# ScalarE begins the transfer of the negated maxima; a transpose, the second statistics and the variance, and one Rsqrt move forward; the maxima of two banks in one reduction

## The chip, the cores and the metric

The kernel runs on one core of a Trainium2 chip. The metric is the device time of one execution in microseconds (us). Five engines work side by side, each in the order of its own program, and wait for one another through semaphores: TensorE (PE in the rows; PEld is its weight load), VectorE (DVE), ScalarE (ACT), GpSimd (POOL) and SyncE (SP), which here does nothing but begin DMA transfers.

## What is computed

The input is `x` of 4 images x 96 channels x 128 x 128, float32. Two layers follow one another. The first is a window attention beside a depthwise convolution:

```python
x = layernorm2d(x0, ln_w, ln_b)
qk = conv1x1(x, qk_w, qk_b)
vs = conv1x1(x, vs_w, vs_b)
local = depthwise_conv3x3(vs, depth_w) + depth_b
v1, v2 = (vs[:, :ADIM], vs[:, ADIM:])
# q, k, v1 are rolled by half a window and cut into windows of 8 x 8 pixels, 4 heads
atn = softmax(einsum('nhqc,nhkc->nhqk', qw, kw) * SCALE)
yw = einsum('nhqk,nhkc->nhqc', atn, vw)
y = concatenate([from_windows(yw), v2], axis=1)
s = (y + local).mean(axis=(2, 3))
ca = sigmoid(conv1x1(leaky_relu(conv1x1(s, fu1_w), 0.2), fu2_w))
x = conv1x1(y * ca + local * (1.0 - ca), proj_w, proj_b) + x0
```

The second is a depthwise convolution with four taps (those above and to the left of the pixel), whose filters are computed from the mean of each channel of that `x`, plus a bias. The gate `ca` and these filters need the means over a whole image, so an image's second half of work can begin only when its first half is through.

## The kernel before

An image is cut into 16 strips of 8 rows, 64 strips in all. A strip passes through an attention half (layer norm, keys, queries, values, scores, softmax) and, 17 strips later (`LAG`), through a second half that applies gate, convolution taps, projection and the second layer. So the program has three stages: strips with the attention half only (the functions called `alone`), strips that do the attention half of strip t+1 and t+2 and the second half of strip t-17 (the functions called `strip`, 48 of them), and a tail with the second half only. Each engine has its own version of these functions, and the order of the calls in them is the order of its work; no scheduler changes it. The strips whose numbers begin and end an image also compute the gate (`gate`, `gated`).

The softmax subtracts the row maximum inside the matmul. `scores` (L521) computes the scores of a strip into the two banks `banks_s`, half of the windows at a time (r = 0, 1). VectorE's `maxima` (L1009) reduces each half. `max_transposed` (L535) turns the 128x32 maxima on TensorE, ScalarE's `maxima_out` (L806) negates them into `nmx`, and `move_max` (L281) on SyncE moves `nmx` by a DMA of 16 KB into four partitions of the query operand `qd`. `scores_transposed` (L529) uses these as extra rows, so that the exponential (`exps`, L811) needs no bias. It waits for the DMA by the semaphore `mx_moved`.

In `strip`, TensorE's order is: `x_transposed` of chunk 0 (L471), the wait for `mx_moved`, `scores_transposed` 0 (L529), `vs_of` (L496, which waits for VectorE's `finish`, L1204, to have read the same bank), `y_transposed` (L541), `scores_transposed` 1, `x_transposed` of chunk 1, `keys_queries` (L504), `values` half 0 (L558), `rstd_rows` (L483), then `scores` 0, `project` 0 (L612, L614), `scores` 1, `values` half 1, `max_transposed`, `project` 1, `v_transposed` (L510), `project_mixed` (L619). ScalarE's is: `exps` 0, `vs_out` twice (L780), `y_out` (L799, which reads what `y_transposed` wrote), `exps` 1, `keys` (L767), `rsqrt` (L758, L762, which reads VectorE's `var`), `queries` (L773), then `tap0`, `sum_x`, `maxima_out`, `first` (L837, the first tap of the next strip) and `values` (L789). VectorE's holds the layer-norm statistics (L980, two chunks), `variance` (L986 to L994), six convolution taps `mix` (L1181), three taps `l1` (L1192), `finish`, `divide`, `normalise` (L1001) and `maxima`. SyncE begins a strip's loads (`load_strip`, L311 to L320, among them `x` by L320) just ahead of `move_max`.

Of the kernel before, what the change touches and what calls it, by code (L numbers as in the profile page):

```python
# [26 lines left out]
ALU = mybir.AluOpType  # L27
# [56 lines left out]
def program(nc, x, out, w):  # L84
    ctx = ExitStack()
    with ctx:
# [179 lines left out]
        def _(sp):  # L266
# [78 lines left out]

            def strip(h, k, attend=True, y=True, ahead=False, prev=False, older=False, gate=None):

# [20 lines left out]
                if ahead:  # L368
                    load_strip(t - LAG + 1, k, prev, gate)
                if attend:  # L370
                    move_max(t + 1, 1 - k)

            strip(0, 0, y=False)
            strip(0, 1)
            with sp.Fori(1, NS // 2) as h:
                strip(h, 0)
                strip(h, 1)
            sp.wait_ge(rim_stored, 16 * 2 * B)
# [84 lines left out]
        def _(pe):  # L463
# [69 lines left out]
            def max_transposed(s):  # L533
                pe.wait_ge(mx_done, 4 * (s + 1))
                nc.tensor.transpose(ps_mx, mx[:].rearrange("q t h p -> q (t h p)"), ident[:]).then_inc(mt_done, 1)  # L535
# [55 lines left out]
            scores(0, 0)  # L591
            pe.wait_ge(mx_done, 2)
            scores(0, 1)
# [28 lines left out]
            def alone(h, k, y=True):  # L622
# [19 lines left out]
                values(t, k, 0, not y)  # L642
                pe.wait_ge(mx_done, 4 * (t + 1) + 2)
                scores(1 - k, 1)
# [5 lines left out]
            def strip(h, k, attend=True, y=True, cur=False, prev=False, gate=None, gated=None, tail=False):  # L650
# [3 lines left out]
                if attend:  # L654
                    x_transposed(t + 2, k, h + 1, 0)
                    pe.wait_ge(mx_moved, 16 * (t + 1))
                    pe.wait_ge(yq_done, FREE + 2 * t)
                    scores_transposed(k, 0)
                    if prev:
                        pe.wait_ge(zs_done, u)  # L660
                    vs_of(t + 1)
                elif prev:
                    pe.wait_ge(zs_done, u - 1 if tail and gated is None else u)
# [10 lines left out]
                if attend:  # L674
                    x_transposed(t + 2, k, h + 1, 1)
                    keys_queries(t + 1)
# [16 lines left out]
                if attend:  # L693
                    pe.wait_ge(mx_done, 4 * (t + 1) + 2)
                    scores(1 - k, 1)
# [51 lines left out]
        def _(act):  # L747
# [54 lines left out]

            def maxima_out(s):
                act.wait_ge(mt_done, s + 1)
                act.wait_ge(mx_moved, 16 * s)
                fn(nmx[:], ps_mx, ACT.Copy, scale=-1.0).then_inc(nmx_done, 1)  # L806

            def exps(t, r):
# [97 lines left out]
            def strip(h, k, attend=True, y=True, ahead=False, prev=False, gate=None, gated=None):  # L906
# [8 lines left out]
                if attend:  # L915
                    exps(t, 1)
                    if gated is not None:
                        sigmoid_exp(gated)
                    keys(t + 1, 1 - k)
                    rsqrt(t + 2)  # L920
                    queries(t + 1, 1 - k)
# [11 lines left out]
                if attend:  # L933
                    maxima_out(t + 1)
                if ahead:
# [35 lines left out]
        def _(dve):  # L971
# [32 lines left out]
            def maxima(s, r):  # L1004
                dve.wait_ge(s_done, 2 * s + r + 1)
                if r == 0 and not (isinstance(s, int) and s == 0):
                    dve.wait_ge(mt_done, s)
                for n in range(2):
                    v.tensor_reduce(mx[:, n, :, 4 * r:4 * r + 4].rearrange("q h e -> q e h"),  # L1009
                                    banks_s[:, n, :].rearrange("q (e h k) -> q e h k", h=2, k=K),  # L1010
                                    AX.X, ALU.max).then_inc(mx_done, 1)

# [223 lines left out]
            def strip(h, k, attend=True, cur=False, prev=False, gate=None, gated=None, tail=False):  # L1236
# [6 lines left out]
                if cur:  # L1243
                    mix(u, par, 0, tail)
                    mix(u, par, 1, tail)
                if gated is not None and attend:
                    leaky(gated)
                if cur:
                    mix(u, par, 2, tail)
                if attend:  # L1250
                    statistics(t + 2, 1)
                    variance(t + 2)
                if gated is not None and attend:
# [118 lines left out]
```

## Time and profile before

| what | value |
|---|---|
| median of three runs | 1500.32 us (1500.12 to 1502.79) |
| the profiled execution, its own time | 1503.79 us |
| its span, from the first to the last instruction | 1502.2 us |
| granted TensorE clock, mean | 0.984 |
| busy: PE, DVE, ACT, POOL | 88%, 84%, 58%, 15% of the span |

The profiled execution is one execution, 3.5 us longer than the median; every duration below is from it. Shares of the span average over three stages that have different limits, so the stage of the 48 strips is looked at by itself. An engine is idle when its next instruction waits for something; the profile names what ended that wait. A busy share says little where an engine is long idle for one thing and then is itself waited for.

### The profile page before, as it was taken

How to read it: one execution, taken by the hardware profiler on the slowest of the kernel's cores; microseconds unless marked ns; L12 is line 12 of the kernel's file. 1: busy time of each engine (PE TensorE's matmuls, PEld its weight loads, DVE VectorE, ACT ScalarE, POOL GpSimd, SP SyncE). 2: the span in 40 equal slices, each digit the busy share in tenths (PEclk: the TensorE clock that was granted, in tenths of full speed). 3: DMA queues.
4: the chain of work that ended last, by engine and by line, in shares of the span. 5: the costliest groups of instructions: out<-in, count | busy, mean ns of one | idle time of the engine just before them, and what ended most of it. 6: DMA issues, size and time to landing. Idle time of an engine off the chain costs nothing.

```text
span 1502.2 us, 38208 instructions
## 1 busy us (share of the span) xinstructions
PE 1323.6 (88%) x12403; PEld 782.0 (52%) x12403; DVE 1263.8 (84%) x2222; ACT 875.8 (58%) x2279; POOL 230.8 (15%) x741
## 2 busy tenths in 40 slices
PE   5989898889899999989899999988989998888986
PEld 3666666555555555555555555555555555433332
DVE  3565656479999999999999999999989998999998
ACT  2566666666666666776566666765666666622221
POOL 2111111111122211221111211220112011000000
PEclk9999999999999999999999999999999999999999
DMA  2121212345665566645655566646655664678884
GB/s 62 51 82 55 81 55 81 99 98 148 167 148 144 138 152 165 156 114 154 166 147 139 138 159 156 156 114 159 155 125 141 161 155 112 164 181 195 211 199 126
DMA packets 81357, 203.07 MB, mean 135 GB/s; under 512 B 15248, under 2 KB 19112, under 8 KB 81320
## 3 DMA queue, kind: packets, MB, share of 16 engines
q1 hardware_dynamic: 81320, 202.60, 53.9%
q8 instruction: 20, 0.33, 0.1%
q14 instruction: 17, 0.14, 0.0%
HBM read 136.57 MB, written 64.91 MB: 134 GB/s over the span
## 4 chain that ended last, share of the span: by engine, by line
PE 36%; ACT 20%; DVE 16%; issue 13%; DMA 13%; ACTq 1%; DVEq 0%; SPq 0%; POOL 0%; POOLq 0%
DMA qd<-nmx 12%; PE banks_s L521 9%; ACT pt L811 5%; PE banks_t L529 5%; PE banks_t L483 5%; ACT km L767 4%; DVE mx L1009 4%; ACT ybuf L799 4%; PE banks_g L612 4%; PE banks_g L496 4%; DVE mixed L1181 3%; PE banks_g L614 3%; DVE oo L1192 3%; ACT vw L780 2%; DVE zs L1204 2%
## 5 line engine op out<-in xcount | busy, mean ns | idle before, releaser
L1181 DVE SCALAR_TENSOR_TENSOR mixed<-vin,c_pack,mixed 96x1024 f32<-96x1024 f32 x352 | 450.0, 1278 | 6.6
L1192 DVE SCALAR_TENSOR_TENSOR oo<-zs,l_w,oo 96x1024 f32<-96x1024 f32 x192 | 245.1, 1276 | 8.3 <-ACT oo L847 4.1
L811 ACT ACTIVATE pt<-banks_t 128x512 f32<-128x512 f32 x256 | 138.6, 593 | 129.0 <-PE banks_t L529 127.5
L1009 DVE TENSOR_REDUCE mx<-banks_s 128x8 f32<-128x512 f32 x260 | 167.6, 687 | 48.1 <-PE banks_s L521 47.3
L529 PE MATMUL banks_t<-qd,km 64*128 64x128 f32 x2048 | 152.8, 290 | 30.1 <-DMA qd<-nmx 30.0
L521 PE MATMUL banks_s<-km,qd 64*128 64x128 f32 x2080 | 152.9, 286 | 18.9 <-issue 15.2
L980 DVE BATCH_NORM_STATS2 bn<-banks_a 128x6 f32<-128x96 f32 x528 | 99.0, 249 | 80.5 <-PE banks_a L471 80.1
L521 PEld LDWEIGHTS banks_s<-km,qd 64*128 64x128 f32 x2080 | 129.7, 189 | 70.7 <-DVE mx L1009 40.4
L612 PE MATMUL banks_g<-vin,proj_t 128*96 128x512 f32 (+1 forms) x288 | 150.2, 622 | 11.4 <-DMA ycat<-y_img 5.7
L529 PEld LDWEIGHTS banks_t<-qd,km 64*128 64x128 f32 x2048 | 127.9, 192 | 49.9 <-issue 26.1
L434 POOL COPY vrow<-vw 96x16 f32<-96x16 f32 (+2 forms) x520 | 153.4, 349 | 0.0
L847 ACT ACTIVATE oo<-zs,c_pack,l_w 96x1024 f32<-96x1024 f32 x64 | 79.0, 1235 | 125.7 <-DVE zs L1204 125.7
L429 POOL TENSOR_TENSOR idle<-idle 96x1 f32<-96x1 f32 x65 | 34.2, 527 | 767.2 <-ACT vw L780 767.2
L789 ACT ACTIVATE vd<-banks_a 64x192 f32<-64x192 f32 x260 | 86.8, 334 | 109.9 <-PE banks_a L510 104.8
L496 PE MATMUL banks_g<-xn,c_pack 96*96 96x512 f32 x260 | 136.6, 650 | 5.7 <-DVE zs L1204 4.4
L504 PE MATMUL banks_g<-xn,w_qk 96*32 96x512 f32 x1040 | 126.8, 605 | 0.0
L483 PE MATMUL banks_t<-ident,rstd 128*96 128x128 f32 x528 | 72.2, 281 | 50.0 <-ACT rstd L762 31.7
L614 PE MATMUL banks_g<-ycat,proj_c 128*96 128x512 f32 x224 | 115.3, 596 | 0.0
L619 PE MATMUL banks_g<-mixed,proj_m 128*96 128x512 f32 x224 | 109.2, 610 | 1.6 <-DVE mixed L1181 1.6
L806 ACT ACTIVATE nmx<-banks_s 32x128 f32<-32x128 f32 x48 | 12.8, 266 | 163.4 <-PE banks_s L535 163.4
L780 ACT ACTIVATE vw<-banks_g,vs_bias 96x512 f32<-96x512 f32 x130 | 88.6, 682 | 27.2 <-PE banks_g L496 22.9
L799 ACT ACTIVATE ybuf<-banks_a 48x256 f32<-48x256 f32 x256 | 93.9, 370 | 4.2 <-PE banks_a L541 2.7
(148 smaller groups left out, 1842.5 us busy)
## 6 DMA issues: line engine op xcount, KB each, us to landing
vin<-v_img SPq DMA_DIRECT2D x64, 495.0 KB, 5.9
v_img<-vrow SPq DMA_DIRECT2D x130, 198.0 KB, 2.8
xc<-in_x SPq DMA_DIRECT2D x134, 192.0 KB, 2.6
x<-in_x SPq DMA_DIRECT2D x64, 384.0 KB, 7.2
out<-oo SPq DMA_DIRECT2D x64, 384.0 KB, 3.0
y_img<-ybuf SPq DMA_DIRECT2D x128, 99.0 KB, 2.0
ycat<-v_img SPq DMA_DIRECT2D x64, 198.0 KB, 4.9
ycat<-y_img SPq DMA_DIRECT2D x64, 198.0 KB, 7.0
```

The source lines that it names most:

```text
L434: nc.gpsimd.tensor_copy(dst.rearrange("c r (p x) -> c p r x", x=min(WS, src.shape[-1])), src).then_inc(vrow_done, 1)
L483: last = nc.tensor.transpose(bc_bank(c)[:C, j * W:(j + 1) * W], rstd[:, at:at + 1].to_broadcast([128, C]), ident[:])
L496: mm(banks_g[:C, w, :], wvs[:], windows(w), start=True, stop=True).then_inc(vs_done, 1)
L521: last = mm(banks_s[:, t, e * 128:(e + 1) * 128], operand(qd, t, k, p), operand(km, t, k, p), start=True, stop=True, tile_position=(64 * t ...
L529: last = mm(banks_t[:, n, e * 128:(e + 1) * 128], operand(km, n, k, p), operand(qd, n, k, p), start=True, stop=True, tile_position=(64 * n ...
L612: mm(z, proj_t[:rows, n, :], vin[:rows, par, at:at + 4, 1 + dw:1 + dw + W], start=n == 0, stop=False)
L614: mm(z, proj_c[:], ycat[:, par, 4 * c:4 * c + 4, 0:W], start=False, stop=False)
L799: fn(dst, src[:, :, wi, :, :], ACT.Copy, accum_out=ystat[0:A, bass.ds(4 * t + 2 * g + wi, 1)]).then_inc(y1_done, 1)
L811: fn(pt[:, 2 * r + n, :], banks_t[:, n, :], ACT.Exp).then_inc(pt_done, 1)
L1009: v.tensor_reduce(mx[:, n, :, 4 * r:4 * r + 4].rearrange("q h e -> q e h"), banks_s[:, n, :].rearrange("q (e h k) -> q e h k", h=2, k=K), ...
L1181: v.scalar_tensor_tensor(out=mb[:C, par, :, 0:W], in0=vin[:C, par, 1 + dh:1 + dh + WS, 1 + dw:1 + dw + W], scalar=depth_w[:, DVE_TAPS[m]:D ...
L1192: v.scalar_tensor_tensor(out=oo[:, par, :, :], in0=zs[:, at:at + WS, 1 + dw:1 + dw + W], scalar=l1_w[:, n:n + 1], in1=oo[:, par, :, :], op ...
```

## The change

Four edits are made in the stage of the 48 strips, and one of them (the reduction) in the first stage too.

- SyncE no longer begins the transfer `qd<-nmx` there. ScalarE begins it, directly behind the instruction that writes `nmx`, after a wait for that instruction's own completion. In the first stage SyncE goes on doing it.
- On VectorE, `statistics` of chunk 1 and `variance` stand ahead of the third tap (`mix` 2), and in strips with a gate ahead of `leaky`; TensorE's `x_transposed` of chunk 1 stands behind `vs_of`, ahead of `y_transposed`, instead of behind `scores_transposed` 1.
- On ScalarE, `rsqrt` stands ahead of `keys` instead of between `keys` and `queries`.
- `maxima` reduces both banks in one instruction, and the counts that others wait for on `mx_done` are halved.

```diff
@@ SyncE: move_max only in the first stage
-                if attend:
+                if attend and alone:
                     move_max(t + 1, 1 - k)
@@ TensorE: strip
                     vs_of(t + 1)
+                    x_transposed(t + 2, k, h + 1, 1)
...
                 if attend:
-                    x_transposed(t + 2, k, h + 1, 1)
                     keys_queries(t + 1)
...
-                    pe.wait_ge(mx_done, 4 * (t + 1) + 2)
+                    pe.wait_ge(mx_done, 2 * (t + 1) + 1)
@@ ScalarE: maxima_out, strip
-            def maxima_out(s):
+            def maxima_out(s, k):
                 act.wait_ge(mt_done, s + 1)
                 act.wait_ge(mx_moved, 16 * s)
                 fn(nmx[:], ps_mx, ACT.Copy, scale=-1.0).then_inc(nmx_done, 1)
+                act.wait_ge(nmx_done, s + 1)
+                act.dma_start(qd[62:66, k, :, :, :].rearrange("j p w q -> j (p w q)"), nmx[:]).then_inc(mx_moved, 16)
...
+                    rsqrt(t + 2)
                     keys(t + 1, 1 - k)
-                    rsqrt(t + 2)
                     queries(t + 1, 1 - k)
@@ VectorE: maxima, strip
-                for n in range(2):
-                    v.tensor_reduce(mx[:, n, :, 4 * r:4 * r + 4].rearrange("q h e -> q e h"),
-                                    banks_s[:, n, :].rearrange("q (e h k) -> q e h k", h=2, k=K),
-                                    AX.X, ALU.max).then_inc(mx_done, 1)
+                v.tensor_reduce(mx[:, :, :, 4 * r:4 * r + 4].rearrange("q n h e -> q n e h"),
+                                banks_s[:, :, :].rearrange("q n (e h k) -> q n e h k", h=2, k=K),
+                                AX.X, ALU.max).then_inc(mx_done, 1)
...
                 if cur:
                     mix(u, par, 0, tail)
                     mix(u, par, 1, tail)
+                if attend:
+                    statistics(t + 2, 1)
+                    variance(t + 2)
                 if gated is not None and attend:
                     leaky(gated)
                 if cur:
                     mix(u, par, 2, tail)
-                if attend:
-                    statistics(t + 2, 1)
-                    variance(t + 2)
```

On TensorE, the loop of the 48 strips from `project_mixed` to `keys_queries` stands in the program before as follows (`ident,xc` are the transposes of `x`, `qd,km` is `scores_transposed`, `xn,c_pack` is `vs_of`, `ident,yq` is `y_transposed`):

```order
L619 MATMUL banks_g<-mixed,proj_m 96x512 x2
L471 MATMUL banks_a<-ident,xc 128x96 x4
L656 REGISTER_ALU
L529 MATMUL banks_t<-qd,km 128x128 x8
L496 MATMUL banks_g<-xn,c_pack 96x512 x2
L541 MATMUL banks_a<-ident,yq 128x128 x4
L529 MATMUL banks_t<-qd,km 128x128 x8
L469 REGISTER_ALU
L471 MATMUL banks_a<-ident,xc 128x96 x4
L504 MATMUL banks_g<-xn,w_qk 32x512 x4
```

The same place in the changed program:

```order
L619 MATMUL banks_g<-mixed,proj_m 96x512 x2
L471 MATMUL banks_a<-ident,xc 128x96 x4
L656 REGISTER_ALU
L529 MATMUL banks_t<-qd,km 128x128 x8
L496 MATMUL banks_g<-xn,c_pack 96x512 x2
L469 REGISTER_ALU
L471 MATMUL banks_a<-ident,xc 128x96 x4
L538 REGISTER_ALU
L541 MATMUL banks_a<-ident,yq 128x128 x4
L671 REGISTER_ALU
L529 MATMUL banks_t<-qd,km 128x128 x8
L504 MATMUL banks_g<-xn,w_qk 32x512 x4
```

The second group of four transposes of `x` has moved ahead of `y_transposed` and of `scores_transposed` 1; `keys_queries` has the same work ahead of it as before.

On ScalarE, the same loop from the end of `y_out` to `values` in the program before (`km` is `keys`, `lnv` and `rstd` are `rsqrt`, `qd` is `queries`):

```order
L801 ACTIVATE ybuf<-banks_a 48x8x4
L811 ACTIVATE pt<-banks_t 128x512 x2
L767 ACTIVATE km<-banks_g,k_bias,k_scale 128x8x64 x2
L757 REGISTER_ALU
L758 ACTIVATE lnv<-var,eps 128x8
L761 REGISTER_ALU
L762 ACTIVATE rstd<-lnv 128x8
L773 ACTIVATE qd<-banks_g,q_bias,q_scale 128x8x64 x2
...
L806 ACTIVATE nmx<-banks_s 32x128
L837 ACTIVATE mixed<-vin,c_pack 96x8x128
L789 ACTIVATE vd<-banks_a 64x16x12 x4
```

and in the changed program:

```order
L801 ACTIVATE ybuf<-banks_a 48x8x4
L813 ACTIVATE pt<-banks_t 128x512 x2
L757 REGISTER_ALU
L758 ACTIVATE lnv<-var,eps 128x8
L761 REGISTER_ALU
L762 ACTIVATE rstd<-lnv 128x8
L767 ACTIVATE km<-banks_g,k_bias,k_scale 128x8x64 x2
L773 ACTIVATE qd<-banks_g,q_bias,q_scale 128x8x64 x2
...
L806 ACTIVATE nmx<-banks_s 32x128
L808 DMA qd<-nmx 4x8x128
L839 ACTIVATE mixed<-vin,c_pack 96x8x128
L789 ACTIVATE vd<-banks_a 64x16x12 x4
```

The two short activations of `rsqrt` now come before `keys`, and the DMA stands between the negated maxima and the first tap.

## Rows read from the trace of the kernel before

**Rows 1.** Windows: stage of 48 strips; busy us of PE, PEld, DVE, ACT, POOL, clock, DMA

```profile
300.00:1303.00 1003.00, 906.10 (x8922) 542.80 (x8920) 917.23 (x1570) 649.21 (x1674) 177.88 (x517) 0.99 0.59 145
```

**Rows 2.** Chain that ended last, pieces of the transfer: start us, us, what

```profile
279.18 2.00 DMA qd<-nmx
...
299.53 3.23 DMA qd<-nmx
...
702.79 4.36 DMA qd<-nmx
```

**Rows 3.** Waits, whole run: us in total, times, longest us

```profile
PE banks_t L529 <- DMA qd<-nmx: 30.0, 40, 2.5
```

**Rows 4.** Timeline, one strip, SyncE and ScalarE: start us, us, engine, [idle before <-releaser]

```profile
701.62 0.32 SPq L320 DMA_DIRECT2D x<-in_x  x1
...
702.79 0.69 SPq L281 DMA_DIRECT2D qd<-nmx  x1
...
708.48 1.08 ACT L811 ACTIVATE pt<-banks_t 128x512 f32<-128x512 f32 x2 [2.28 <-PE banks_t L529]
```

**Rows 5.** Timeline, TensorE, first matmuls of `scores_transposed` 0 in five strips

```profile
348.92 1.16 PE L529 MATMUL banks_t<-qd,km 64*128 64x128 f32 x16
...
369.27 1.16 PE L529 MATMUL banks_t<-qd,km 64*128 64x128 f32 x16
...
390.63 1.16 PE L529 MATMUL banks_t<-qd,km 64*128 64x128 f32 x16 [0.60 <-DMA qd<-nmx]
...
707.27 1.16 PE L529 MATMUL banks_t<-qd,km 64*128 64x128 f32 x16 [0.30 <-DMA qd<-nmx]
...
727.90 1.16 PE L529 MATMUL banks_t<-qd,km 64*128 64x128 f32 x16 [0.18 <-DMA qd<-nmx]
```

**Rows 6.** Timeline, strip of 348.92: `y_transposed`, `x_transposed` 1, first `y_out`

```profile
351.83 0.60 PE L541 MATMUL banks_a<-ident,yq 128*128 128x128 f32 x4
...
353.45 0.55 PE L471 MATMUL banks_a<-ident,xc 96*128 96x96 f32 x4
...
352.78 0.36 ACT L799 ACTIVATE ybuf<-banks_a 48x256 f32<-48x256 f32 x1
```

**Rows 7.** Timeline, strip of 369.27: `vs_of` on TensorE

```profile
370.74 1.50 PE L496 MATMUL banks_g<-xn,c_pack 96*96 96x512 f32 x3 [0.30 <-DVE zs L1204]
```

**Rows 8.** Timeline, ScalarE: the strip where `y_out` waits for `y_transposed`

```profile
1270.06 0.38 ACT L799 ACTIVATE ybuf<-banks_a 48x256 f32<-48x256 f32 x1 [0.19 <-PE banks_a L541]
```

**Rows 9.** Timeline, strip of 369.27: three taps, end of the variance, `exps` 1

```profile
371.08 3.90 DVE L1181 SCALAR_TENSOR_TENSOR mixed<-vin,c_pack,mixed 96x1024 f32<-96x1024 f32 x3
...
376.60 0.17 DVE L994 SCALAR_TENSOR_TENSOR var<-m,diff 128x8 f32<-128x8 f32 x1
...
375.25 1.08 ACT L811 ACTIVATE pt<-banks_t 128x512 f32<-128x512 f32 x2
```

**Rows 10.** Groups by line: out<-in, shapes, xcount | busy us, mean ns | idle before

```profile
L1009 DVE TENSOR_REDUCE mx<-banks_s 128x8 f32<-128x512 f32 x260 | 167.6, 687 | 48.1 <-PE banks_s L521 47.3
L980 DVE BATCH_NORM_STATS2 bn<-banks_a 128x6 f32<-128x96 f32 x528 | 99.0, 249 | 80.5 <-PE banks_a L471 80.1
```

**Rows 11.** Timeline, VectorE, one pair of reductions

```profile
380.98 1.28 DVE L1009 TENSOR_REDUCE mx<-banks_s 128x8 f32<-128x512 f32 x2
```

**Rows 12.** Timeline, strip of 536.52, TensorE ahead of `scores` 0

```profile
545.45 1.07 PE L483 MATMUL banks_t<-ident,rstd 128*96 128x128 f32 x8 [0.66 <-ACT rstd L762]
546.83 1.16 PE L521 MATMUL banks_s<-km,qd 64*128 64x128 f32 x16 [0.31 <-issue]
```

**Rows 13.** Timeline, TensorE, `scores_transposed` 0 after long waits

```profile
281.22 2.08 PE L529 MATMUL banks_t<-qd,km 64*128 64x128 f32 x16 [1.36 <-DMA qd<-nmx]
...
1047.72 1.16 PE L529 MATMUL banks_t<-qd,km 64*128 64x128 f32 x16 [1.32 <-DMA qd<-nmx]
...
1263.23 2.08 PE L529 MATMUL banks_t<-qd,km 64*128 64x128 f32 x16 [2.07 <-DMA qd<-nmx]
```

**Rows 14.** Windows, TensorE alone: us, PE busy, granted clock, DMA share, GB/s

```profile
1263.20:1270.00 6.80, 6.77 (x26) 0.50 0.01 3
```

More of the change, by code:

```diff
@@ L344, in _, with strip @@
             move_max(0, 0)
-            def strip(h, k, attend=True, y=True, ahead=False, prev=False, older=False, gate=None):
+            def strip(h, k, attend=True, y=True, ahead=False, prev=False, older=False, gate=None, alone=False):
                 t = 2 * h + k
@@ L369, in strip @@
                     load_strip(t - LAG + 1, k, prev, gate)
-                if attend:
+                if attend and alone:
                     move_max(t + 1, 1 - k)
-            strip(0, 0, y=False)
-            strip(0, 1)
+            strip(0, 0, y=False, alone=True)
+            strip(0, 1, alone=True)
             with sp.Fori(1, NS // 2) as h:
-                strip(h, 0)
-                strip(h, 1)
+                strip(h, 0, alone=True)
+                strip(h, 1, alone=True)
             sp.wait_ge(rim_stored, 16 * 2 * B)
@@ L533, in max_transposed @@
             def max_transposed(s):
-                pe.wait_ge(mx_done, 4 * (s + 1))
+                pe.wait_ge(mx_done, 2 * (s + 1))
                 nc.tensor.transpose(ps_mx, mx[:].rearrange("q t h p -> q (t h p)"), ident[:]).then_inc(mt_done, 1)
@@ L591, in _ @@
             scores(0, 0)
-            pe.wait_ge(mx_done, 2)
+            pe.wait_ge(mx_done, 1)
             scores(0, 1)
@@ L693, in strip @@
                 if attend:
-                    pe.wait_ge(mx_done, 4 * (t + 1) + 2)
+                    pe.wait_ge(mx_done, 2 * (t + 1) + 1)
                     scores(1 - k, 1)
@@ L933, in strip @@
                 if attend:
-                    maxima_out(t + 1)
+                    maxima_out(t + 1, 1 - k)
                 if ahead:
```

## The prediction

> **What bounds the kernel now.** I read the windows first. The four edits lie in the stage of the 48 strips, which lasts 1003 us [rows 1], 20.9 us a strip. VectorE is busy 917 of them, the most of the engines beside TensorE's 906, but neither is full: there must be a loop of waits that sets the period. So I read next the chain that ended last. In a strip it goes through the transfer `qd<-nmx`, 4.36 us from SyncE's issue to TensorE's start [rows 2]. The waits' list puts a price on it: TensorE stood still for it 40 times, 30.0 us in all, 2.5 at the longest [rows 3]. That is much less than 4.36 us a strip, because TensorE has the rest of the strip before to finish while the transfer is under way. Only what is left over costs time.
>
> Then I asked what a strip takes when the transfer is not waited for. The strip that begins at 348.92 takes 20.35 us to 369.27; the next takes 21.36 to 390.63, of which 0.60 is a wait at its end, so 20.76 [rows 5]. Both began without a wait. A strip that began with a wait, 707.27 to 727.90, takes 20.63 less 0.18, so 20.45 [rows 5]. The difference is the next thing in line: in the strip of 369.27 `vs_of` waits 0.30 for VectorE to have read its bank [rows 7]; a strip whose `scores_transposed` is itself late does not meet this wait. So a strip without the transfer's wait costs 20.56 on the mean of both kinds, and one with a wait of g costs 20.45 + g.
>
> The reader is to see that 30 us is the most that a faster transfer can give back of itself, and that not all of it comes, since the next wait is already there.
>
> **The change, part by part.**
>
> *The transfer.* With SyncE it takes 2.00 us from issue to use at the end of the first stage, 3.23 in the first strip of the second, 4.36 in a later strip [rows 2]. SyncE issues it right away (702.79), but 1.2 us behind the load of `x` [rows 4], one of seven loads of the strip on the same queue. The length of it grows with what lies ahead on that queue, and from ScalarE's queue nothing does. I bound it by 2.00 and 4.36 and take 3.2, the row between: the 16 DMA engines are still shared with the loads. At 707.27 a landing 0.30 earlier would have cost no wait [rows 5], so anything up to 4.06 is as good as 2.0. Of the 30.0 us I take off 1.4 for the strip of 281.22 [rows 13], whose transfer SyncE still begins, and 2.5 for the strip after it, which waits even at 3.2. There remain 26.1 us in 38 strips.
>
> The Trainium skill's page "DMA: Bandwidth & Descriptors" (section "Queues, rings and completion order") says that SP and ACT each own one ring on every DMA engine and that an engine takes the rings in turn, packet by packet. By that the transfer would be next in turn and land near the short rows; no run here has a second ring in use to show it.
>
> ScalarE pays for the issue: 0.69 on SyncE [rows 4]. Behind it stand `first`, `values` and then `exps` 0, ahead of which ScalarE idles 2.28 [rows 4]. So it is hidden; without that cover it would be 0.69 a strip, 33 us over the stage.
>
> *The transposes ahead of `y_transposed`.* This costs. In the strip of 348.92 `y_transposed` ends at 352.43 and `y_out` begins at 352.78 [rows 6]. Four transposes of 0.55 put the end at 352.98. If ScalarE begins then, it is 0.20 late; in the one strip where `y_out` had to wait it began 0.19 after ScalarE was free [rows 8], which makes 0.39. ScalarE's work from `y_out` to `queries` has no gap, so `scores` and the whole loop move with it. I take 0.35, near that one row; the bounds are 0.20 and 0.39.
>
> *Statistics, variance and `rsqrt` earlier.* The variance ends at 376.77; with the third tap (3.90 / 3 = 1.30) behind it, it ends at 375.47, before `exps` 1 ends at 376.33 [rows 9]. So ScalarE need not wait, and the same activations run in another order: nothing. `rstd_rows` no longer waits 0.66, but `scores` needs `queries`, which is no sooner: nothing gained. In three strips with a gate `leaky` now stands 1.8 later (from the taps' end at 374.97 to 376.77) and TensorE's second gate matmul with it; `keys_queries` queues behind that, yet ScalarE needs it only after `exps` 1. Bounds 0 and 1.8 a strip, I take 0.3, so 0.9.
>
> *One reduction for two.* No row has a reduction over 1024. From 96 to 512 columns the mean goes from 249 to 687 ns [rows 10], 1.05 ns a column, so 1024 give 687 + 539 = 1.23 us; the pair takes 1.28 [rows 11]. Bounds: nothing, and 0.6 (the second reduction wholly gone). I take 0.06, once a strip: after the second reduction TensorE waits for it; after the first TensorE is still busy with `project`. In the 16 strips of the first stage it stands on the loop too: 1.0 us.
>
> *The clock.* After the wait of 2.07 TensorE ran at 0.50 of its clock, 1.2 instead of 2.4 GHz, for 6.8 us with 6.77 busy [rows 13, 14]; half of that, 3.4 us, was lost. Without the wait it comes back; I take 3.0.
>
> *The sum.* A strip becomes 20.56 + 0.35 - 0.06 = 20.85. VectorE can follow: with the same work it did a strip in 20.35. The 38 waiting strips lose their 26.1 us and pay 20.85 - 20.45 = 0.40 each, 15.2; the nine others pay 0.29 each, 2.6. So 26.1 - 15.2 - 2.6 = 8.3; with 3.0 for the clock, 1.0 for the first stage and 0.9 off for the gates it is 11.4 us. The profiled execution took 1503.79, 1.6 more than its span, so it would take 1492.4. It is 3.5 us above the median; I carry the difference over to the median: 1500.3 - 11.4 = 1488.9, about **1489 us**. A measurement of this kernel tells about 0.2%, 3 us, from no change.
>
> **The rivals.**
>
> *A, slower: the transfer lands no sooner.* Then every strip keeps its wait and pays for the transposes: 47 x (0.35 - 0.06) = 13.6, and 0.9 - 1.0 for gates and first stage: 1514; at the lower bound of 0.20 it is 6.6 and 1507. For it: the same DMA engines carry the loads, and their backlog may be what takes the time. Against it: 2.00 and 4.36 differ by what SyncE queued. It decides at a landing 0.35 us sooner on the mean (13.5 / 38). The Trainium skill speaks for this rival: the same page, section "Issuing engines are not separate DMA queues", says that transfers begun by different engines run on the same 16 engines and interleave, and that beginning them on several only saves issue time.
>
> *B, slower: TensorE's clock falls at the new gap.* Today TensorE waits 0.66, does `rstd_rows`, and waits 0.31 ahead of `scores` [rows 12]. With `rstd` early and `queries` 0.35 later it waits 1.3 in one piece. A wait of 1.32 kept the clock (1.16 us for the same matmuls), one of 1.36 did not (2.08) [rows 13]. Each fall costs up to 3.4 us [rows 14]; from some four to seven strips on it eats the gain. In one strip of six, at 2.5 us, 1489 + 20 = 1509.
>
> *C, faster: the transposes cost 0.20 and the clock gives all 3.4.* A strip is then 20.70; 26.1 - 38 x 0.25 - 9 x 0.14 = 15.3, with 3.4 and 1.0 it is 19.7: 1481.
>
> *D, the transfer lands only a little sooner*, 4.36 less 0.3: 38 x 0.3 = 11.4 against 13.5 of costs, 1502.
>
> **How the numbers follow.** The forecast has 0.45; its own range, with the bounds of the small terms, is 1482 to 1494. C has 0.15, D 0.10, A 0.13 and B 0.17 (with times from 1495 up). Faster by over 0.2% (below 1497.3): the forecast, C, a little of B and D (0.03 each), 0.66. Within it: the rest of D and some of B, 0.11. Slower (above 1503.3): A and most of B, 0.23. The range leaves out the best part of C and the top of A and B: 1479 to 1509.
>
> **What the changed profile would show.** The transfer under ScalarE, 2 to 4 us from issue to TensorE's start, and the wait of `scores_transposed` for it near 4 us in total instead of 30.0. `vs_of` waiting for VectorE in every second strip. `y_out` waiting for `y_transposed` in most strips, which it did not do. One wait ahead of `scores` 0 in place of two, and the granted clock there. One reduction of about 1.23 us. Starts of `scores_transposed` 0 about 20.85 apart. It would be wrong if the transfer's wait stays, if the granted clock falls in many strips, or if ScalarE's issue holds `first` and `values` longer than 2.28 us.

## The result: slower by 0.9%

| what | before | after |
|---|---|---|
| median, four runs each | 1500.32 us (1500.12 to 1502.79) | 1513.54 us (1512.62 to 1515.81) |
| the profiled execution | 1503.79 us | 1512.62 us |
| its span | 1502.2 us | 1510.8 us |

The ratio is 1.0087, with a 95% interval of 1.0069 to 1.0104: 13 us slower, where 11 us faster was forecast. It is the time of rival A (1514).

First, where the time went. The first matmuls of `scores_transposed` 0 (TensorE's timeline) bracket the stage of the 48 strips. Before:

```profile
302.81 1.01 PE L529 MATMUL banks_t<-qd,km 64*128 64x128 f32 x6 [2.50 <-DMA qd<-nmx]
...
1287.34 0.93 PE L529 MATMUL banks_t<-qd,km 64*128 64x128 f32 x11 [0.68 <-DMA qd<-nmx]
```

and after:

```profile
301.75 2.08 PE L529 MATMUL banks_t<-qd,km 64*128 64x128 f32 x16 [2.62 <-DMA qd<-nmx]
...
1297.14 1.05 PE L529 MATMUL banks_t<-qd,km 64*128 64x128 f32 x14 [1.15 <-DMA qd<-nmx]
```

Between them lie 46 strips: 984.5 us before, 995.4 after, 10.9 more. Ahead of them the program is 1.1 us shorter, behind them 1.2. That is the 8.6 by which the two spans differ, so the whole loss lies in the strips.

The windows of that stage, in the columns of [rows 1]:

```profile
300.00:1303.00 1003.00, 886.61 (x8804) 536.30 (x8808) 901.78 (x1461) 649.48 (x1661) 230.21 (x512) 0.99 0.58 143
```

TensorE and VectorE are busy for less of the same stretch, at the same granted clock: more waiting, not more work. The list of waits says which (us in total, times, longest):

```profile
DVE mx L1010 <- PE banks_s L521: 68.7, 105, 1.6
PE banks_s L521 <- issue: 63.0, 46, 1.4
...
PE banks_t L529 <- DMA qd<-nmx: 31.1, 35, 2.6
```

The reader is to see two things. The wait that the change should have removed is still there: 31.1 us against 30.0 [rows 3]. And ahead of `scores` (L521) TensorE now stands still for 63.0 us in 46 waits; before, it was 15.2 there and 31.7 ahead of `rstd_rows`, 46.9 in all, of which one wait of 2.1 is left. So there are 18 us more, and VectorE's `maxima` wait for that. A strip grows by less than that, as the experiments show. `issue` means that the profile names nothing that the engine waited for; here it is ScalarE's `queries`, 0.10 us behind whose end `scores` begins.

The transfer in one strip of the changed kernel, the same one as in [rows 4] (timeline of SyncE, ScalarE and TensorE):

```profile
703.01 0.32 SPq L320 DMA_DIRECT2D x<-in_x  x1
704.04 0.27 ACT L806 ACTIVATE nmx<-banks_s 32x128 f32<-32x128 f32 x1 [3.50 <-PE banks_s L535]
704.34 0.64 ACTq L808 DMA_DIRECT2D qd<-nmx  x1
705.08 1.16 ACT L839 ACTIVATE mixed<-vin,c_pack 96x1024 f32<-96x1024 f32 x1 [0.77 <-DMA vin<-v_img]
...
709.50 1.16 PE L529 MATMUL banks_t<-qd,km 64*128 64x128 f32 x16 [0.94 <-DMA qd<-nmx]
```

ScalarE issues it at 704.34 and TensorE starts at 709.50, 5.16 us later with 0.94 of waiting. The first of its packets starts at 707.31. Until shortly before that, the 16 DMA engines are busy all the time, as the window from the issue on shows (us, PE busy, clock, DMA share, GB/s):

```profile
704.34:706.95 2.61, 2.61 (x14) 1.00 1.01 206
```

It does run on a queue of its own, as the list of queues shows (packets, MB, share of the engines' span):

```profile
q1 hardware_dynamic: 79592, 201.82, 53.1%
q10 hardware_dynamic: 1728, 0.79, 0.3%
```

Each transfer is 32 packets of 512 bytes. From the packet records of the two traces, mean over the 45 transfers between 340 and 1300 us, counted from the issue: the first packet starts after 2.65 us before and 2.61 after; the last ends after 4.04 and 4.01; TensorE starts after 4.82 and 4.87. The other queue changed nothing. In the strips where the load of `x` (96 packets) is issued less than 3 us ahead, 34 in each trace, hardly any of these packets have started when SyncE issues the transfer; when its first packet starts, 69 have on the mean, and when its last starts, 94. From ScalarE's queue it is 67 and 94: on a queue of its own the transfer gets no further ahead of a load that was begun before it.

The same strip a little later (TensorE and ScalarE) shows the cost of the transposes:

```profile
712.38 0.49 PE L471 MATMUL banks_a<-ident,xc 96*128 96x96 f32 x4
712.72 0.60 PE L541 MATMUL banks_a<-ident,yq 128*128 128x128 f32 x4
713.26 0.19 ACT L780 ACTIVATION_READ_ACCUMULATOR vw<-banks_g,vs_bias  x1
713.55 0.38 ACT L799 ACTIVATE ybuf<-banks_a 48x256 f32<-48x256 f32 x1
...
718.19 1.44 ACT L773 ACTIVATE qd<-banks_g,q_bias,q_scale 128x512 f32<-128x512 f32 x2
719.73 1.16 PE L521 MATMUL banks_s<-km,qd 64*128 64x128 f32 x16 [1.41 <-issue]
```

`y_transposed` ends at 713.32 and `y_out` begins at 713.55, 0.10 after ScalarE was free (713.45); and the two waits of [rows 12] have become one of 1.41. `queries` ends at 719.63 and `scores` begins at 719.73.

### The profile page after: what moved, and what is told of

Its sections match the earlier page's. It is cut to its first block, busy times and chain, and to the rows that moved or that the text cites. A ratio compares the mean times of both kernels' runs of the same rounds, so it can differ in the third digit from the quotient of the medians.

```text
span 1510.8 us, 38078 instructions
## 1 busy us (share of the span) xinstructions
PE 1309.5 (87%) x12403; PEld 779.0 (52%) x12403; DVE 1255.6 (83%) x2092; ACT 882.5 (58%) x2279; POOL 287.2 (19%) x741
## 4 chain that ended last, share of the span: by engine, by line
PE 56%; DVE 18%; DMA 12%; issue 10%; ACT 4%; DVEq 0%; ACTq 0%; SPq 0%; POOL 0%; POOLq 0%
DMA qd<-nmx 11%; PE banks_s L521 9%; PE banks_g L496 8%; PE banks_t L529 8%; PE banks_g L504 7%; DVE mx L1010 5%; PE banks_g L612 4%; PE banks_t L483 4%; PE banks_a L558 4%; PE banks_g L614 4%; DVE mixed L1182 3%; DVE oo L1193 3%; DVE zs L1205 2%; PE banks_a L541 2%; PE banks_a L471 2%
## 5 line engine op out<-in xcount | busy, mean ns | idle before, releaser
L434 POOL COPY vrow<-vw 96x16 f32<-96x16 f32 (+2 forms) x520 | 224.8, 488 | 0.0
L1010 DVE TENSOR_REDUCE mx<-banks_s 128x16 f32<-128x1024 f32 x130 | 159.3, 1225 | 69.7 <-PE banks_s L521 68.7
L521 PE MATMUL banks_s<-km,qd 64*128 64x128 f32 x2080 | 153.7, 287 | 66.4 <-issue 63.0
L521 PEld LDWEIGHTS banks_s<-km,qd 64*128 64x128 f32 x2080 | 130.5, 190 | 118.1 <-issue 79.2
L529 PE MATMUL banks_t<-qd,km 64*128 64x128 f32 x2048 | 151.4, 288 | 31.2 <-DMA qd<-nmx 31.1
L429 POOL TENSOR_TENSOR idle<-idle 96x1 f32<-96x1 f32 x65 | 12.5, 192 | 785.7 <-ACT vw L780 785.7
L496 PE MATMUL banks_g<-xn,c_pack 96*96 96x512 f32 x260 | 133.4, 637 | 5.8 <-DVE zs L1205 4.5
L839 ACT ACTIVATE mixed<-vin,c_pack 96x1024 f32<-96x1024 f32 x64 | 74.1, 1158 | 48.9 <-DMA vin<-v_img 36.7
```

What stands on the lines that cost most here:

```text
L434: nc.gpsimd.tensor_copy(dst.rearrange("c r (p x) -> c p r x", x=min(WS, src.shape[-1])), src).then_inc(vrow_done, 1)
L496: mm(banks_g[:C, w, :], wvs[:], windows(w), start=True, stop=True).then_inc(vs_done, 1)
L521: last = mm(banks_s[:, t, e * 128:(e + 1) * 128], operand(qd, t, k, p), operand(km, t, k, p), start=True, stop=True, tile_position=(64 * t ...
L529: last = mm(banks_t[:, n, e * 128:(e + 1) * 128], operand(km, n, k, p), operand(qd, n, k, p), start=True, stop=True, tile_position=(64 * n ...
L1010: v.tensor_reduce(mx[:, :, :, 4 * r:4 * r + 4].rearrange("q n h e -> q n e h"), banks_s[:, :, :].rearrange("q n (e h k) -> q n e h k", h=2 ...
```

## The experiments

All times are medians; the runs of before beside them, on the same chip, are given with each group. Where a load is moved behind the transfer, a few lines are added, and line numbers shift by six (by eight where ScalarE begins the transfer too): there `scores_transposed` is L535, `y_transposed` L547, `y_out` L805, `scores` L527, `max_transposed` L541. "A strip" is the distance between two starts of `scores_transposed` 0. The theories are these. Theory 1: the transfer waits for what is already under way on the DMA engines, which all queues share; so the queue gains nothing, and the transposes cost. Theory 2: an edit costs by itself, by ScalarE's issue or by the order of the statistics. Theory 3: the transfer's length is its own.

### One part at a time

Before: 1503.49 us, 23 runs.

**Only ScalarE's transfer.** Edit: SyncE's `move_max` only in the first stage, ScalarE's `dma_start` in `maxima_out`, as in the change.

> Only the first edit: ScalarE begins the transfer qd<-nmx in the stage of the 48 strips; the rest as before. Theory 1 (the transfer waits behind the loads on the DMA engines, whatever queue it comes from, and the loss of the whole change is the later scores): from ScalarE's issue to TensorE's start 4.8 us as before, the wait of scores_transposed for it 28 to 32 us, time within 3 us of before. Theory 2 (ScalarE's issue is what costs, since the first tap and the values stand behind it): 8 us or more slower than before, with the first tap waiting for the negated maxima in many strips.

Measured: 1504.31 us, ratio 1.0005 (0.9985 to 1.0025). TensorE's start comes 4.94 us after the issue. The waits:

```profile
PE banks_t L529 <- DMA qd<-nmx: 36.0, 40, 2.9
...
ACT mixed L839 <- ACT nmx L806: 14.6, 18, 0.9
```

The wait, at 36.0 us, is longer than the 28 to 32 expected, but not shorter: the other queue buys nothing. ScalarE's issue holds the first tap 18 times, 14.6 us, and that costs nothing either: theory 2 falls for this edit.

**Only the reordering.**

```diff
                     vs_of(t + 1)
+                    x_transposed(t + 2, k, h + 1, 1)
...
-                    x_transposed(t + 2, k, h + 1, 1)
...
+                    rsqrt(t + 2)
                     keys(t + 1, 1 - k)
-                    rsqrt(t + 2)
...
                     mix(u, par, 1, tail)
+                if attend:
+                    statistics(t + 2, 1)
+                    variance(t + 2)
```

> Only the second and third edits: statistics 1 and variance ahead of the third tap, x_transposed 1 behind vs_of, rsqrt ahead of keys; the rest as before. Theory 1: y_out begins behind y_transposed, one wait of about 1.3 us ahead of scores 0 in place of two that sum to 1.0, so 0.35 us a strip and 13 to 17 us slower than before. Theory 2: the order costs little, within 4 us of before.

Measured: 1523.63 us, ratio 1.0151 (1.0126 to 1.0177), more than theory 1's 13 to 17 us. The wait ahead of `scores` is that of the whole change, 62.6 us, 46 times. The loss comes from here; which of its three moves it is was still open.

**Only the reduction.** Edit: the one `tensor_reduce` of the change, with the counts on `mx_done` halved.

> Only the fourth edit: one reduction over both banks; the rest as before. Theory 1: one reduction takes 1.225 us where two took 1.28 to 1.37, so 2 to 6 us faster than before (0.05 to 0.1 us in each of 64 strips). Theory 2: the reduction can no longer begin with the first bank alone and the transposed maxima come later: 2 us or more slower.

Measured: 1504.34 us, ratio 1.0009 (0.9990 to 1.0029): no change that the time shows, and neither theory's 2 us. The one instruction is as short as forecast (groups by line):

```profile
L1008 DVE TENSOR_REDUCE mx<-banks_s 128x16 f32<-128x1024 f32 x130 | 159.2, 1224 | 51.5 <-PE banks_s L521 50.6
```

**The load of `x` behind the transfer**, all else as before, SyncE's transfer too.

```diff
                 sp.dma_start(ycat[0:A, par, :, :], y_img[...])
-                if prev:
-                    sp.wait_ge(zs_done, before)
-                sp.dma_start(x0[:, par, :, :], x[...])
...
                 if attend:
                     move_max(t + 1, 1 - k)
+                if ahead:
+                    load_x0(t - LAG + 1, k, prev)
```

> The kernel before, with the load of x (384 KB, begun 1.2 us ahead of the transfer) begun behind the transfer on SyncE; the transfer stays on SyncE. Theory 1 (what is already under way on the shared DMA engines sets the landing): from issue to TensorE's start under 4.2 us in place of 4.8 and the wait for the transfer below 15 us in all; since a strip without that wait meets the next one 0.1 later, 8 to 20 us faster. Theory 3 (the length of the transfer is its own, 32 packets of 512 bytes and their completion): 4.8 us still, the same time.

Measured: 1476.63 us, ratio 0.9846 (0.9822 to 0.9870), 27 us faster, more than the 8 to 20 expected. SyncE's timeline in a strip:

```profile
692.75 0.32 SPq L317 DMA_DIRECT2D ycat<-y_img  x1
694.57 0.69 SPq L281 DMA_DIRECT2D qd<-nmx  x1
695.53 0.33 SPq L324 DMA_DIRECT2D x<-in_x  x1
```

TensorE's wait for the transfer, in the list of waits:

```profile
PE banks_t L535 <- DMA qd<-nmx: 4.3, 6, 1.4
```

and TensorE's starts in three strips in a row:

```profile
386.06 1.16 PE L535 MATMUL banks_t<-qd,km 64*128 64x128 f32 x16
...
406.42 1.16 PE L535 MATMUL banks_t<-qd,km 64*128 64x128 f32 x16
...
427.12 1.16 PE L535 MATMUL banks_t<-qd,km 64*128 64x128 f32 x16
```

The wait of 30 us has shrunk to 4.3, the transfer's last packet ends 2.34 us after the issue instead of 4.04, none of the strips from 324.00 on has the lower clock (before, those of 1112.32 and 1263.23 had), and the strips take 20.36 and 20.70 in turn. Nothing about the queue was changed, only what was under way ahead of the transfer. Theory 3 falls.

### With the transfer early

Now that the transfer's wait is out of the way, the other terms can be seen by themselves. Before: 1501.83 us, 18 runs.

**The other three edits, with the load of `x` behind SyncE's transfer.**

> The load of x behind the transfer, the transfer on SyncE, and the other three edits (transposes and statistics, rsqrt, one reduction). The transfer is then early, so this measures the other terms of the prediction's sum. Theory 1 (their sum is 0.29 us a strip, as predicted): strips of about 20.85 us with hardly a wait for the transfer, 0.9 to 1.0% slower than with the load of x moved alone, that is a ratio near 0.993 to before. Theory 2 (they cost 0.4 us and more by themselves, as their own run gave 1.5%): a ratio of 0.998 or more.

Measured: 1497.60 us, ratio 0.9963 (0.9944 to 0.9982), between the two theories. Three starts in a row, and the strip of 387.63 in detail:

```profile
387.63 1.16 PE L535 MATMUL banks_t<-qd,km 64*128 64x128 f32 x16
...
390.87 0.60 PE L547 MATMUL banks_a<-ident,yq 128*128 128x128 f32 x4
391.40 0.19 ACT L786 ACTIVATION_READ_ACCUMULATOR vw<-banks_g,vs_bias  x1
391.68 0.38 ACT L805 ACTIVATE ybuf<-banks_a 48x256 f32<-48x256 f32 x1
...
397.85 1.16 PE L527 MATMUL banks_s<-km,qd 64*128 64x128 f32 x16 [1.37 <-issue]
...
408.23 1.16 PE L535 MATMUL banks_t<-qd,km 64*128 64x128 f32 x16
...
429.19 1.16 PE L535 MATMUL banks_t<-qd,km 64*128 64x128 f32 x16
```

`y_out` begins 4.05 us after `scores_transposed` (391.68 - 387.63) and `scores` 10.22; with the load of `x` moved alone these are 3.87 and 10.02:

```profile
388.97 0.60 PE L547 MATMUL banks_a<-ident,yq 128*128 128x128 f32 x4
...
389.93 0.36 ACT L805 ACTIVATE ybuf<-banks_a 48x256 f32<-48x256 f32 x1
...
396.08 1.16 PE L527 MATMUL banks_s<-km,qd 64*128 64x128 f32 x16 [0.31 <-issue]
```

(counted from 386.06). So 0.18 of `y_out`'s delay arrives as 0.20 at `scores`. (`y_transposed` begins 3.24 after `scores_transposed`, against 2.91: four more transposes ahead of it move its start by 0.33, less than their row is long; in the changed strip above that row lasts 0.49, and the next one begins 0.34 after it.) Strips take 20.60 and 20.96, 20.78 on the mean, 0.25 more than with the load alone: 47 x 0.25 = 12 us. Besides, three strips at a granted clock of 0.92 take 22.2 to 22.6, some 1.3 to 1.6 more than their like, and the one that begins at 637.16, with a gate, takes 28.0 at 0.82, 3.9 more. Together this is 20 us, about the distance of 1.2% (18 us).

**ScalarE's transfer, the load of `x` behind it.**

```diff
+                if attend:
+                    sp.wait_ge(first_done, held(u + 1))
                 if prev:
                     sp.wait_ge(zs_done, before)
                 sp.dma_start(x0[:, par, :, :], x[...])
```

> The load of x behind the transfer, as before begun by SyncE, but the transfer begun by ScalarE; SyncE begins the load of x when the first tap is through, behind ScalarE's issue. Theory 1 (what is under way on the shared DMA engines sets the landing, the queue does nothing): first packet 1.2 to 1.5 us after the issue, the wait for the transfer under 8 us, the same time as with SyncE's transfer, a ratio of 0.98 to 0.99 to before. Theory 2 (ScalarE's issue costs by itself): a ratio of 0.995 or more.

Measured: 1476.69 us, ratio 0.9833 (0.9817 to 0.9849); the first packet starts after 1.33 us, the wait is 3.5 us in all, twice. With either engine the transfer is late when `x` goes ahead and early when it goes behind. Theory 1 holds in all four corners.

**Only the transposes, with the load of `x` behind.** Edit: the move of `x_transposed` 1 as above, and no other.

> The load of x behind the transfer, and only x_transposed 1 ahead of y_transposed; statistics, rsqrt and reductions as before. Theory 1 (the transposes make y_out late, and that is the cost of the reordering): strips of 20.8 to 21.0 us, a ratio of 0.992 to 1.000 to before. Theory 2 (the cost lies in the statistics or in rsqrt): strips of 20.55 us, a ratio of 0.983 to 0.987.

Measured: 1493.35 us, ratio 0.9939 (0.9916 to 0.9962). TensorE's starts:

```profile
391.00 1.16 PE L535 MATMUL banks_t<-qd,km 64*128 64x128 f32 x16
...
411.55 1.16 PE L535 MATMUL banks_t<-qd,km 64*128 64x128 f32 x16
...
432.46 1.16 PE L535 MATMUL banks_t<-qd,km 64*128 64x128 f32 x16
```

Strips take 20.55 and 20.91, 0.2 more than with the load of `x` alone, 9.4 us in 47 strips; that is a little under the strips of theory 1. Four strips at a clock of 0.92 to 0.93 take 22.6 to 23.1, 1.6 to 2.0 more than their like, which covers the other 4.6. So most of the loss is this one move.

**Only the reduction, with the load of `x` behind.**

> The load of x behind the transfer, and one reduction for two. Theory 1 (0.06 us a strip and as much in the first stage): strips of 20.5 us, a ratio of 0.980 to 0.984 to before, 2 to 5 us faster than with the load moved alone. Theory 2: VectorE's maxima hold nothing up, the same as with the load moved alone (0.985).

Measured: 1479.32 us, ratio 0.9849 (0.9827 to 0.9872), the same as with the load alone (0.9846). From the start of `scores` 1 to `max_transposed`, the place where the reduction stands on the loop, 2.58 us pass with one reduction (396.79 to 399.37) and 2.55 with two (399.06 to 401.61, load of `x` alone). It is a shorter instruction, and the matmul behind it starts no sooner. The strips show more than the medians can: 20.42 and 20.77 against 20.36 and 20.72 (medians of the strips at full clock without a wait for the transfer), 0.05 to 0.06 longer. The same shows with the transfer late: strips that begin with a wait, taken without the wait at their end, have a median of 20.47 in the run with only the reduction against 20.41 before. So one instruction for two costs a little, some 2.5 us in 47 strips, too little for the medians of the runs to show.

### The place of the transposes, and how much load

Before: 1501.90 us, 17 runs.

**All three edits, but the transposes behind `y_transposed`.**

```diff
                 if y:
                     y_transposed(t - 1)
+                if attend:
+                    x_transposed(t + 2, k, h + 1, 1)
...
                     scores_transposed(k, 1)
...
-                    x_transposed(t + 2, k, h + 1, 1)
```

> The load of x behind the transfer, SyncE's transfer, one reduction, statistics and variance ahead of the third tap, rsqrt ahead of keys, but x_transposed 1 behind y_transposed instead of ahead of it (still ahead of scores_transposed 1). Theory 1 (the whole cost of the reordering is that y_out starts late): y_out no longer waits, strips of 20.5 to 20.6 us, a ratio of 0.982 to 0.987. Theory 2 (the early statistics cost too, or the one long wait ahead of scores 0 drops TensorE's clock by itself): a ratio of 0.989 or more, with strips at a granted clock near 0.92.

Measured: 1478.67 us, ratio 0.9833 (0.9816 to 0.9850), strips of 20.4 and 20.8. In TensorE's timeline `rstd_rows` no longer waits, and the wait ahead of `scores` is one of 1.18:

```profile
731.19 1.07 PE L489 MATMUL banks_t<-ident,rstd 128*96 128x128 f32 x8
733.45 1.16 PE L527 MATMUL banks_s<-km,qd 64*128 64x128 f32 x16 [1.18 <-issue]
```

That is the strip of the run with the reduction alone, so the early statistics and `rsqrt` are free, and worth nothing. What cost was that `x_transposed` stood ahead of `y_transposed`.

**Half of the load of `x` ahead, half behind.** Edit: two `dma_start` of four rows each, the second behind `move_max`.

> Half of the load of x (192 of 384 KB) begun ahead of the transfer as before, half behind it, all by SyncE. Theory 1 (the bytes that are under way on the shared engines set the landing): first packet about 2.0 us after the issue, between 2.65 with all of it ahead and 1.35 with none; the wait for the transfer 5 to 20 us; a ratio of 0.985 to 0.992. Theory 3 (it is the neighbouring issue on SyncE, not the bytes): first packet 2.5 us or later, the time of before.

Measured: 1483.56 us, ratio 0.9873 (0.9854 to 0.9891), the wait 11.8 us, 26 times, both as theory 1 has it; the first packet starts sooner than it said, after 1.71 us. Since `x` is still issued just ahead of the transfer here, it is the bytes and not the neighbouring issue.

**`x` and `y_img` behind.** Edit: the `dma_start` of `ycat` from `y_img` moved into `load_x0`, too.

> The load of x (384 KB) and that of ycat from y_img (198 KB) both behind the transfer on SyncE. Theory 1: first packet under 1.2 us after the issue, but TensorE waits no more than the 4 us that were left, so the same time as with x alone, a ratio of 0.982 to 0.987; project may wait longer for y_img.

Measured: 1476.55 us, ratio 0.9826 (0.9810 to 0.9842), the wait 2.6 us, twice. Together with the earlier runs this makes a row of doses. The packet columns are mean us after the issue, 45 transfers each:

| begun ahead of the transfer, of `x` and `y_img` | first packet starts | last ends | TensorE's wait in all | ratio to before |
|---|---|---|---|---|
| 384 + 198 KB (before) | 2.65 | 4.04 | 30.0 | 1 |
| the same, ScalarE's queue alone | 2.64 | 4.14 | 36.0 | 1.0005 |
| 192 + 198 KB | 1.71 | 3.39 | 11.8 | 0.9873 |
| 198 KB | 1.35 | 2.34 | 4.3 | 0.9846 |
| 198 KB, ScalarE's queue | 1.33 | 2.24 | 3.5 | 0.9833 |
| neither | 1.32 | 1.73 | 2.6 | 0.9826 |

The fewer the bytes ahead, the sooner it lands, on either queue. The first packet did not come under 1.2 us, as expected for the last row: in the last three rows it stays near 1.3.

**`scores` 0 ahead of `rstd_rows`,** a try at a faster version, with the load of `x` behind.

```diff
                     keys(t + 1, 1 - k)
-                    rsqrt(t + 2)
                     queries(t + 1, 1 - k)
+                    rsqrt(t + 2)
...
-                    rstd_rows(t + 2, 0)
-                    rstd_rows(t + 2, 1)
...
                     scores(1 - k, 0)
+                    rstd_rows(t + 2, 0)
+                    rstd_rows(t + 2, 1)
...
+                    maxima(t + 1, 0)
                     normalise(t + 2, k, 0)
                     normalise(t + 2, k, 1)
-                    maxima(t + 1, 0)
```

> The load of x behind the transfer, and the reverse of the third edit: rsqrt behind queries, rstd_rows behind scores 0 on TensorE, normalise behind maxima 0 on VectorE. Theory 1 (with the transfer early the loop runs through ScalarE's row from exps 0 to queries and on to scores 0): queries 0.5 us earlier, strips of 20.1 to 20.4 us, a ratio of 0.970 to 0.980. Rival (VectorE is full at 0.94 and normalise comes later there): strips of 20.55 us or longer, a ratio of 0.984 or more.

Measured: 1508.74 us, ratio 1.0038 (1.0023 to 1.0054), slower even than before. That is outside theory 1 and within the rival's bounds, but not for the rival's reason, as the rows show. TensorE's timeline, `scores` 0 in one strip, then the next strip from its start to `scores` 1:

```profile
679.20 2.08 PE L527 MATMUL banks_s<-km,qd 64*128 64x128 f32 x16 [1.54 <-issue]
...
691.90 1.16 PE L535 MATMUL banks_t<-qd,km 64*128 64x128 f32 x16
...
701.42 1.16 PE L527 MATMUL banks_s<-km,qd 64*128 64x128 f32 x16 [1.53 <-issue]
702.51 1.07 PE L489 MATMUL banks_t<-ident,rstd 128*96 128x128 f32 x8
...
705.23 1.16 PE L527 MATMUL banks_s<-km,qd 64*128 64x128 f32 x16
```

The windows of the first of these, of the matmuls from 679.20 on and of the whole strip (us, PE busy, granted clock, DMA share, GB/s):

```profile
679.20:682.30 3.10, 3.10 (x21) 0.50 0.82 250
...
669.00:691.90 22.90, 20.36 (x190) 0.93 0.55 139
```

`scores` does begin sooner, 9.5 us after `scores_transposed` (701.42 less 691.90) in place of 10.0. But `rstd_rows`, 1.07 us that had filled the wait for `queries`, now stands behind it, and the wait is an empty one of 1.5. `scores` 1 begins 3.81 after `scores` 0 (705.23 less 701.42), where it was 2.98 (399.06 less 396.08, load of `x` alone), and waits for nothing: 0.5 gained, 0.8 lost, on TensorE itself and not by VectorE. Strips take 20.7 and 21.0, and in 14 of them the clock falls, which makes 22.4 to 24.9.

## Why the prediction was wrong, point by point

**What bounds the kernel: right.** The transfer is waited for 30 us, and a strip without that wait takes 20.35 and 20.76 in turn: the runs with the load of `x` behind show 20.36 and 20.70 to 20.77. By the prediction's numbers a faster transfer alone was to give 26.1 less 0.11 in each of 38 strips (20.56 against 20.45), 22, and 3.0 for the clock, 25 us. The moved load gave that: 46 strips take 959.6 us in its profile where they take 984.5 before, 24.9 less, and by the medians it is 27 us. One reading was loose: 4.36 us is the time to the landing; TensorE starts at 707.27 [rows 5], 4.48 after the issue.

**The transfer: the step that failed.** The prediction said that its length "grows with what lies ahead on that queue, and from ScalarE's queue nothing does", and took 3.2 us. The rows it rested on, 2.00, 3.23 and 4.36 us [rows 2], do grow with what SyncE had begun. But that is what a backlog on the shared engines would show as well, as the prediction itself said of rival A; nothing in the rows told the two apart, and rival A got 0.13. The runs do. From issue to use it is 4.82 us before, 4.87 after, 4.94 with that edit alone, 4.21 with `x` behind (where TensorE, no longer waiting, itself sets the start). What the transfer waits for is the loads begun ahead of it, whichever queue it comes from.

The Trainium skill's page "DMA: Bandwidth & Descriptors" has both rules. Its section "Issuing engines are not separate DMA queues" is borne out: 30.0 us of waits before, 31.1 after, on a second queue. What the prediction concluded from "Queues, rings and completion order", where an engine takes its rings in turn, that the transfer would be next, did not happen: the first packet came after 2.61 us where it had been 2.65. Why an otherwise empty queue is not served sooner is not settled by these runs, since the records do not name the engine of a packet.

**ScalarE's issue: hidden, as forecast.** With `x` behind, the time is 1476.69 us with ScalarE's transfer and 1476.63 with SyncE's.

**The transposes: right in kind, smaller.** 0.35 us a strip was taken from the one row of `y_out` waiting [rows 8], with a lower bound of 0.20. With the transfer early it is 0.2: 20.55 and 20.91 against 20.36 and 20.70. Two steps of the working were off, and partly made up for each other: the four transposes move `y_transposed` by 0.33 and not by the 0.55 of their row, and the lower bound left out that `y_out` begins some 0.2 behind `y_transposed`'s end (0.23 in the changed strip above). In the changed kernel the strips that begin with a wait take 20.66 by their median, without the wait at their end, against 20.41 before. 47 x 0.25 = 11.8 us, and with 1.1 us more of the transfer's wait that is about the loss measured.

**Statistics, variance, `rsqrt`: right.** Nothing gained, nothing lost. In the run with the transposes behind `y_transposed`, two strips with a gate take 24.52 and 24.24 us against 24.12 and 24.13 with the load of `x` alone, near the 0.3 forecast for them.

**The reduction: 0.06 a strip gained by forecast, 0.05 lost.** The duration was right (1.225 us measured, 1.23 forecast), but the matmul behind it starts 0.03 later, not sooner (2.58 us against 2.55); where the rest of the 0.05 arises is open. The 1.0 us of the first stage is not shown: the stage of the strips began 1.1 sooner, but in the run with only ScalarE's transfer, whose first stage is that of before, it began 1.5 sooner (301.32 against 302.81).

**The clock: no 3.0 us came back,** as the waits stayed. Rival B's mechanism exists: at about 1.4 us ahead of `scores` the clock mostly holds and sometimes falls. In the changed kernel it fell in the strips of 753.32 and 797.71:

```profile
763.55 2.08 PE L521 MATMUL banks_s<-km,qd 64*128 64x128 f32 x16 [1.42 <-issue]
```

(TensorE's timeline; the same 16 matmuls take 1.16 in [rows 12]), with this window from there on, in the columns of [rows 14]:

```profile
763.55:767.19 3.64, 3.64 (x18) 0.53 0.82 235
```

That is 1.2 GHz for nearly all of 3.64 us, so 1.7 lost. Two such strips are no more than before had of its own, at 1112.32 and 1263.23, so B is not the cause here.

**The sum.** With an early transfer the strips were to take 20.56 + 0.35 - 0.06 = 20.85; the run with three edits and an early transfer has 20.78, which is 20.53 + 0.20 + 0.05. The two small terms were off by 0.15 and 0.11 in opposite directions, so that this sum came out so near, and rival A's 1514 with it, is in part luck. The term that carried the sign is the transfer's. One thing stays open: the reordering alone was 20 us slower by the medians, more than the whole change; its profiled execution, the shortest of its six, had a span 15.4 us longer than that of before. Of these, 11.9 lie in its 46 strips, near the whole change's 10.9; the rest lies ahead of the stage (0.9) and behind it (2.6), where it runs the program of before.

## What to carry to other kernels

A small, urgent transfer was not made sooner by another engine's queue while the DMA engines were full: look at the bytes that were begun ahead of it, and begin the loads that are not needed soon behind it. Where rows fit both "its queue is full" and "the engines are full", they are no evidence for one over the other, and both deserve a like chance; one run that moves a load tells. On an engine, work that fills a wait is free there and costs time elsewhere, so moving it forward or back is priced by what then stands ahead of the loop's next step (here the transposes ahead of `y_transposed`, 0.2 us a strip, and `rstd_rows` ahead of `scores` 1, 0.8 for 0.5 gained).

## What the runs showed of the hardware that was not expected

- One reduction over 1024 columns takes 1.225 us where two over 512 take 1.28, and the matmul that waits for it starts no sooner but 0.03 later (2.58 us against 2.55).
- TensorE's clock after the waits ahead of `scores`: none of 45 single waits of about 1.2 us let it fall, two or three of 46 of about 1.4 did (two in the changed kernel and with the reordering alone, three with the three edits and `x` behind), and with 48 of about 1.5 us 14 strips had it lower. A wait in two pieces did not keep it: with the transposes moved alone, waits of about 1.0 and 0.3 with `rstd_rows` between them, it fell in four strips. After such a fall it was mostly at 1.2 GHz for some 3 us, and a strip took mostly 1.3 to 2.0 us longer.
- GpSimd's copies of `vrow` from `vw` took 349 ns on the mean before and 488 after, the same 520 copies (page, groups by line):

```profile
L434 POOL COPY vrow<-vw 96x16 f32<-96x16 f32 (+2 forms) x520 | 224.8, 488 | 0.0
```

VectorE's new order alone does not explain it: the mean is 506 with the reordering alone, but 395 with the same order and the load of `x` behind, and 396 with only that load moved. What does was not tested.
